# Transformer layer on one core: normalized rows stored and x loaded in tiles of 256 KB, with their places in SyncE's program

## The reference, cut to what matters

```python
x = _ln(src) * (1.0 + scale) + shift            # scale, shift from the timestep
q, k, v = x @ Wq + bq, x @ Wk + bk, x @ Wv + bv # 16 heads of 32
scores = einsum('bhqd,bhkd->bhqk', q / sqrt(32), k) + attention_bias   # bias: 16 x 16 x 512 x 512
probs = softmax(where(src_mask, -inf, scores))
x = x + (probs @ v) @ Wo + bo
h = _ln(x) * g2 + beta2
return x + _gelu2(h @ W1 + b1) @ W2 + b2        # then each group of 4 columns is rotated by theta, phi
```

## Time and profile before

| | |
|---|---|
| median of three runs | 3251.16 us (3250.86 to 3253.52) |
| the profiled execution, its own time | 3257.1 us |
| its span, first to last instruction | 3255.3 us |
| PE busy | 3148.9 us (97%) |
| DVE, POOL, ACT busy | 2146.3, 2015.2, 1864.9 us |
| moved by DMA | 785.15 MB, mean 241 GB/s |

### The profile page before, as it was taken

One profiled execution on the slowest core, in us unless ns is written; L12 is line 12 of the kernel. 1 busy time (PEld: TensorE's weight loads), 2 busy tenths in 40 slices (PEclk: granted clock), 3 DMA queues, 4 the chain that ended last, 5 costly groups with the idle time before them and its releaser, 6 DMA issues. The chain is left out here.

```text
span 3255.3 us, 52383 instructions
## 1 busy us (share of the span) xinstructions
PE 3148.9 (97%) x16592; PEld 2369.6 (73%) x16592; DVE 2146.3 (66%) x4446; ACT 1864.9 (57%) x4057; POOL 2015.2 (62%) x1246
## 2 busy tenths in 40 slices
PE   5999999999999999999969999999999999999998
PEld 4777777777777777777637687787877868687787
DVE  4777778777777777787758664545645465464542
ACT  3777777777777777787744343443424334253433
POOL 3888888898888888888738633334343442434413
PEclk9999999999999999999989999999999999999999
DMA  6988899988999888898757686675867757586665
GB/s 203 271 271 264 255 285 278 271 264 273 261 273 280 266 263 275 268 283 267 233 178 258 228 261 207 205 247 179 261 198 241 230 183 254 176 262 207 198 205 166
DMA packets 440432, 785.15 MB, mean 241 GB/s; under 512 B 57024, under 2 KB 106176, under 8 KB 440160
## 3 DMA queue, kind: packets, MB, share of 16 engines
q1 hardware_dynamic: 440160, 781.82, 77.7%
HBM read 591.76 MB, written 89.19 MB: 209 GB/s over the span
## 5 line engine op out<-in xcount | busy, mean ns | idle before, releaser
L691 POOL TENSOR_TENSOR biasm<-biasm,maskb 128x1024 f32<-128x1024 f32 x512 | 1089.9, 2148 | 199.1 <-DMA biasm<-in_fside_Bx16xSxS_dram 196.5
L1424 PE MATMUL ps_out<-w_ring,g_hi 128*128 128x512 f32 x2048 | 676.8, 397 | 15.9 <-POOL w_ring L1679 7.9
L1404 PE MATMUL ps_first<-h_hi,w_ring 128*128 128x512 f32 x1792 | 553.5, 390 | 6.3 <-issue 6.3
L1661 POOL TENSOR_TENSOR g_lo<-g_now,g_hi 128x512 fp32r<-128x512 f32 x128 | 169.7, 1326 | 606.1 <-ACT g_hi L1523 606.1
L796 PE MATMUL ps_score<-k_rows,q_rows 96*128 96x512 f32 x1024 | 492.7, 481 | 0.1
L1424 PEld LDWEIGHTS ps_out<-w_ring,g_hi 128*128 128x128 f32 x2048 | 384.5, 188 | 110.5 <-issue 31.6
L847 ACT ACTIVATE probT<-ps_probT 128x512 f32<-128x512 f32 x512 | 305.0, 596 | 250.0 <-PE ps_probT L809 162.1
L934 DVE CUSTOM_DVE_ANT_0 prob_last<-ps_score,biasm 128x512 f32<-128x512 f32 x512 | 347.7, 686 | 140.5 <-PE ps_score L796 124.0
L934 DVE CUSTOM_DVE_ANT_0 prob_first<-ps_score,biasm 128x512 f32<-128x512 f32 x512 | 348.5, 685 | 132.4 <-PE ps_score L796 110.8
L809 PE MATMUL ps_probT<-ident,prob_first 128*128 128x128 f32 x2048 | 392.6, 273 | 17.7 <-DVE probT L519 10.1
L1424 PE MATMUL ps_out<-w_ring,g_lo 128*128 128x512 f32 x1024 | 398.8, 389 | 0.0
(11 more groups left out here) (170 smaller groups left out, 5614.4 us busy)
## 6 DMA issues: line engine op xcount, KB each, us to landing
biasm<-in_fside_Bx16xSxS_dram SPq DMA_DIRECT2D x512, 512.0 KB, 6.1
w_ring<-w_parts SPq DMA_DIRECT2D x240, 512.0 KB, 3.8
w_ring<-w_parts SPq DMA_DIRECT2D x392, 256.0 KB, 3.5
k_rows<-k_hi SPq DMA_DIRECT2D x512, 64.0 KB, 5.1
q_rows<-q_hi SPq DMA_DIRECT2D x512, 64.0 KB, 3.2
xn<-in_x_dram SPq DMA_DIRECT2D x16, 1024.0 KB, 6.7
normal_rows<-xn SPq DMA_DIRECT2D x16, 1024.0 KB, 9.0
k_rows<-k_lo SPq DMA_DIRECT2D x256, 64.0 KB, 4.6
```

Source lines behind the costliest of these rows:

```text
L691: pool.tensor_tensor(tile, tile, maskb[:, 2 * half:2 * half + 2, :], ALU.add).then_inc(masked.sem, 1)
L1404: mm = pe.matmul(ps[:, BANK[n], :], w1r[:, place, w, cols], h[:, n, c, :], start=(c == 0 and k == 0 and not onto), stop=(c == 1 and k == 2 ...
L1424: mm = pe.matmul(ps_out[:, t, :], a[:, k % 2, cols], w2r[:, k % VR, w, :], start=(m == 0 and n == 0), stop=(m == NF - 1 and n == 2))
L1661: pool.tensor_tensor(GLO[:, k % 2, :], src, GHI[:, k % 2, :].bitcast(F32), ALU.subtract).then_inc(glo_done.sem, 1)
```

## The change

The load of x and the store of the normalized rows are each cut in four, one DMA a tile of 128 rows (256 KB). The stores stand at slots 22, 23, 24 and 26 (each after `normed` of its own tile), the loads at slots 36, 38, 40 and 41, and the load of the mask moves from slot 44 to 45. `x_in` and `normal_out` count four DMAs (64) for a batch, and those who wait for them wait for all four. The statistics on DVE stay at slots 43, 47, 50 and 59. In the setup the four loads stand one after another.

```diff
-                load_x(sp, 0)
+                for t in range(4):
+                    load_x(sp, 0, t)
...
-    x_in = Tally(sem("x_in"), 1, 16)
+    x_in = Tally(sem("x_in"), 1, 16 * NT)
-    def load_x(sp, b):
-        sp.dma_start(xn[:, :, :], x[bass.ds(b, 1), :, :].rearrange("o (t p) d -> p (o t) d", p=P)).then_inc(x_in.sem, 16)
+    def load_x(sp, b, t):
+        sp.dma_start(xn[:, t, :], x[bass.ds(b, 1), t * P:(t + 1) * P, :].rearrange("o p d -> p (o d)")).then_inc(x_in.sem, 16)
...
-    normal_out = Tally(sem("normal_out"), 1, 16)
+    normal_out = Tally(sem("normal_out"), 1, 16 * NT)
...
-    STORE_AT, LOAD_AT, MASK_AT = 24, 36, 44
+    STORE_AT, LOAD_AT, MASK_AT = (22, 23, 24, 26), (36, 38, 40, 41), 45
...
-                    if slot == STORE_AT and mode in AHEAD:
-                        normed.wait(sp, b, NT - 1)
-                        sp.dma_start(normal_dram[bass.ds(b + 1, 1), :, :].rearrange("o (t p) d -> p (o t) d", p=P),
-                                     xn[:, :, :]).then_inc(normal_out.sem, 16)
-                    if slot == LOAD_AT and b + 2 < B:
-                        xt_done.wait(sp, b, NC - 1)
-                        normal_out.wait(sp, b, 0)
-                        load_x(sp, b + 2)
+                    if slot in STORE_AT and mode in AHEAD:
+                        t = STORE_AT.index(slot)
+                        normed.wait(sp, b, t)
+                        sp.dma_start(normal_dram[bass.ds(b + 1, 1), t * P:(t + 1) * P, :].rearrange("o p d -> p (o d)"),
+                                     xn[:, t, :]).then_inc(normal_out.sem, 16)
+                    if slot in LOAD_AT and b + 2 < B:
+                        t = LOAD_AT.index(slot)
+                        if t == 0:
+                            xt_done.wait(sp, b, NC - 1)
+                            normal_out.wait(sp, b, 0)
+                        load_x(sp, b + 2, t)
```

## The result

The changed kernel takes 3356.47 us (median of four, 3354.87 to 3359.16) against 3251.01 for the kernel before: a ratio of 1.032, 95% interval 1.031 to 1.034. That is 105 us slower; the forecast was 83.

What follows compares the result with a forecast made beforehand. PE was taken to bound the kernel (97% of the span). Stalls of 63 us plus 20 us of clock loss made 83, taking the profiled 3257.1 us to 3340, or 3334 us against the median 3251.2; range 3265 to 3385.

Steps and rivals of the forecast that it cites:

- SP's place in time: SP issuing from slot 36 to 41: the fourth load of x goes out 5.7 us after the first.
- The landing: Load of x: all four pieces complete 12.6 us after the first is issued, between 11.0 and 15.5.
- by bytes: Landing estimated from the bytes queued up to the slot-41 bias load: 12.9 us after the x issue on the mean.
- by the mask: Landing estimated from the 256 KB mask load's 7.5 us, added to 5.7 us of issue: 13.2 us.
- DVE's wait: DVE's first statistics at slot 43, ready at 6.3 us, wait 6.3 us a batch for x, before 0.9.
- PE's cover: Before transpose 45, PE absorbs 1.2 us of DVE's wait and pays the rest one for one: 5.1 us idle.
- What is not lost twice: PE's present waits on copies by DVE and ACT, some 8 us, come off 71 us of stalls: 63 us.
- ACT's wait for the q rows: ACT's 31.3 us behind the big x load would go, bringing nothing beyond the 8 us already taken off.
- The clock: Each 5.1 us PE stall drops the clock to half, charged at 1.4 us a batch, 20 us in all.
- Stores: Four store pieces at slots 22 to 26: data ready, extra issues covered by the bias ring; effect taken as zero.
- The stall without the clock: Rival, chance 0.24: PE stalls as forecast but the clock holds, so only 63 us are added, 3315 us.
- Small transfers pay one after another: Rival, chance 0.04: each load piece pays its whole landing in turn, 7.3 us more a batch, 3436 us.

Runs made afterwards that it cites:

- early_pieces: The changed kernel with its four loads at slots 36, 37, 38 and 39: 3310.99 us, ratio 1.018.
- stats_late: The changed kernel with DVE's four statistics moved to slots 50, 53, 56 and 59: 3252.38 us, ratio 0.9999.
- warm_stall: The changed kernel with 20 extra, unread matmuls on PE ahead of the transpose of slot 45: 3327.80 us, ratio 1.0229.
- size_only: The kernel before with its load in four 256 KB pieces, all at slot 36, store and mask as before: 3261.68 us, ratio 1.0025.
- place_only: The kernel before with its one 1 MB load moved to slot 41 and the mask to 45: 3364.27 us, ratio 1.034.

## Why the prediction was right, step by step

- *SP's place in time.* Fourth piece 5.7 us behind the first: 4.8 to 7.1 in the fourteen batches, mean 5.5. The longest gaps come with long issues: in the one of 7.1 us a bias load took 1.51 us to issue and a row piece 1.78.
- *The landing.* x complete 12.6 us after the first piece: 11.8 to 13.8, mean 12.8. Both ways of estimating it held, 12.9 by bytes and 13.2 by the mask. How near they came is in part luck: the same count of bytes put early_pieces at 9.8, and it measured 10.6.
- *DVE's wait.* 6.3 us a batch: 6.5 (90.6 / 14).
- *PE's cover.* 1.2 us: 5.3 us of stall (74.2 us for the fourteen) for 6.5 of wait, so 1.2, and again 1.2 with early_pieces.
- *What is not lost twice.* PE's named waits went from 16.1 to 81.4 us in the window, 65.3 more, forecast 63. ACT's wait for the q rows went, as said, and brought nothing.
- *The clock: this term was mis-sized.* I charged 1.4 us a batch, 20 us. PE's busy time for the same matmuls grew by 32.7 us, 2.3 a batch, and the run with PE kept at work gave 28.7 us back. The price was read from the restart at 59.71 us, where the clock had fallen at 55.8, 3.9 us before PE went on, so that I saw only some 3 us of slow matmuls. In the changed kernel it falls 0.1 to 3.0 us before PE goes on, and slow work follows for 4.6 us on the mean (784.86 to 790.6 in the batch above). The row behind 4.52 us of idle time was misread too: the clock fell at 1687.3, 0.6 us after PE had gone on at 1686.68, and slow matmuls stood behind the transposes until 1690.9. Followed to its end it would have priced a stall at 1.7 us, 24 us in all, still short of 32.7.
- *Stores.* Zero: a gain of 0.1%, at the edge of the noise. The place of the mask was not tried alone; stats_late includes it and shows no loss.
- *The rivals.* "The stall without the clock" asked for 3315; warm_stall, which is that case made by hand, took 3328: the stalls, with whatever the extra matmuls add, cost some 10 us more than that rival said. "Small transfers pay one after another" fell with size_only.

The sum for the profiled execution was 3340 us and 3357.2 came out: 17 us short, 13 of them the clock and 4 the idle time (67.4 us against 63; 65.3 of it in named waits). The other 5 us of the 105 lie in the profiled execution of before, itself 6 us over its median.

The change moved the last 256 KB of the load 5.5 us closer to a reader that needed none of it yet: the first statistics read tile 0 alone, but wait for the count of all four.

## What to carry to other kernels

When a transfer is cut up or moved later, go to its reader: what counts is when the last byte that the reader's wait asks for lands, measured from the point where the reader is ready, in the real time of the issuing queue and not in slots of the program. In this kernel a wait had a small cover (1.2 us) and was paid in full beyond it, and a stall of a few microseconds on PE was mostly paid a second time in the clock, so follow the slow matmuls to the last one before you price it. Moving the reader seven slots later cost nothing here and undid the whole loss.

## What the hardware did that I had not expected

- The clock can fall after PE has gone back to work: 1.3 us after it, behind a stall of 3.44 us (early_pieces). The Trainium skill ("TensorE: Matmul & The Clock Gate", section "HAM oscillation — how this bites in real kernels") describes kernels that lose the clock at each wait for a DMA; with stalls of 4.34 to 6.21 us that is what happened here, in every one of the fourteen batches, with DVE between the DMA and PE.
- The kernel with 280 more matmuls of 512 columns ran 28.7 us faster than the one without.
- On a busy queue the size of a load says little by itself. The last pieces of 256 KB, issued at slot 41, took 5.9 to 8.1 us to land, and 1 MB at slot 36 before 5.8 to 8.7. Its own bytes count as well, though: 1 MB issued at slot 41 (place_only) took 8.3 to 10.5.
